# A four-layer graph network on one core: gated sums of two destination tiles in one addition, and staging drained as high parts, counts, low parts

## What is computed

```python
h = relu(layernorm(x))
g = sigmoid(h @ W_gate + b_gate)                    # one gate for a node
x = x + segment_sum(edge_weight * (g * (h @ W))[dst], src)     # layer 0, the weighted one
x = x + segment_sum(h[src], dst) @ W1.T + b1                   # layer 1, h of the new x
x = x + concat(h, segment_sum(message(h[src], h[dst]), dst)) @ W_upd + b_upd   # layer 2
x = x + relu(batchnorm(D_inv * A @ (B_inv * A.T @ (h @ W3)) + b3))             # layer 3
```

## Time and profile before

| what | value |
|---|---|
| time, median of 3 runs | 2575.72 us (2571.42 to 2576.82) |
| the profiled execution: its own time | 2590.25 us |
| the profiled execution: span from the first to the last instruction | 2588.4 us |
| the build, as a stretch of the span | 131.8 to 1327 us |
| mean granted TensorE clock | 0.958 of full speed |
| bytes moved by DMA | 589.27 MB, mean 228 GB/s |

### The profile page before, as it was taken

One profiled execution on the slowest core, in us unless ns is written; L12 is line 12 of the kernel. 1 busy time (PEld: TensorE's weight loads), 2 busy tenths in 40 slices (PEclk: granted clock), 3 DMA queues, 4 the chain that ended last, 5 costly groups with the idle time before them and its releaser, 6 DMA issues. The chain is left out here.

```text
span 2588.4 us, 71075 instructions
## 1 busy us (share of the span) xinstructions
PE 2311.7 (89%) x27901; PEld 1993.6 (77%) x27901; DVE 1599.1 (62%) x3654; ACT 1218.6 (47%) x2644; POOL 45.6 (2%) x51
## 2 busy tenths in 40 slices
PE   2489899999989998999938999899998999999997
PEld 2368788878778887887837888788887888887786
DVE  6689999999999998999962333234433222122223
ACT  2478787877778886887732222222232000011112
POOL 3300000000000000000000000000000000000000
PEclk9589999999999999999979999999999999999998
DMA  6579999999999999999999999899997999999997
GB/s 190 110 152 204 208 208 207 215 217 210 201 193 216 213 213 201 196 215 209 207 229 232 283 284 281 227 260 259 260 258 203 290 288 290 274 246 245 256 267 186
DMA packets 1608975, 589.27 MB, mean 228 GB/s; under 512 B 964422, under 2 KB 1605450, under 8 KB 1608567
## 3 DMA queue, kind: packets, MB, share of 16 engines
q1 hardware_dynamic: 1604869, 579.88, 100.7%
q0 software_dynamic: 1600, 4.92, 0.7%
q10 hardware_dynamic: 2226, 0.62, 0.2%
HBM read 255.26 MB, written 89.20 MB: 133 GB/s over the span
## 5 line engine op out<-in xcount | busy, mean ns | idle before, releaser
L1182 ACT CAST stage<-ps 128x784 f16<-128x784 f32 x784 | 656.5, 837 | 108.5 <-DMA counts_by_source<-stage 69.5
L655 PE MATMUL ps<-Ha,a_tiles 128*128 128x258 f16 x4802 | 548.2, 274 | 46.4 <-ACT Ha L1229 38.9
L655 PEld LDWEIGHTS ps<-Ha,a_tiles 128*128 128x128 f16 x4802 | 469.9, 98 | 116.5 <-ACT Ha L1229 39.1
L608 PE MATMUL ps<-hot_c,hot_r 128*128 128x98 f16 x3136 | 509.8, 212 | 13.6 <-DVE hot_c L890 7.3
L609 PE MATMUL ps<-hot_c,hot_r 128*128 128x98 f16 x3136 | 504.1, 211 | 0.0
L610 PE MATMUL ps<-hot_c,hot_r 128*128 128x98 f16 x3136 | 502.3, 210 | 0.0
L1167 ACT CAST stage<-ps 128x392 f16<-128x392 f32 x784 | 398.8, 509 | 141.5 <-PE ps L591 141.5
L583 PE MATMUL ps<-g_in,wt 128*128 128x128 f16 x2401 | 431.4, 222 | 34.7 <-DVE X L902 18.2
L584 PE MATMUL ps<-g_in,wt 128*128 128x128 f16 x2401 | 429.4, 222 | 0.0
L585 PE MATMUL ps<-g_in,wt 128*128 128x128 f16 x2401 | 429.2, 222 | 0.0
L902 DVE SCALAR_TENSOR_TENSOR X<-ps,X 128x512 f32<-128x512 f32 (+1 forms) x637 | 391.6, 649 | 52.1 <-PE ps L585 51.9
(11 more groups left out here) (195 smaller groups left out, 2039.8 us busy)
## 6 DMA issues: line engine op xcount, KB each, us to landing
a_tiles<-counts_by_source SPq DMA_DIRECT2D x147, 1600.0 KB, 8.8
counts_by_source<-stage SPq DMA_DIRECT2D x49, 1600.0 KB, 8.0
gated_parts<-G SPq DMA_DIRECT2D x7, 448.0 KB, 3.6
g_in<-gated_parts SPq DMA_DIRECT2D x98, 32.0 KB, 3.1
out_x<-X SPq DMA_DIRECT2D x12, 256.0 KB
edge_table<-tab SPq DMA_DIRECT2D x1, 2448.0 KB, 10.5
wt<-stage SPq DMA_TRANSPOSE x98, 10.9
dst_run<-in_dst SPq DMA_DIRECT2D x1, 612.4 KB
```

Source lines behind the costliest of these rows:

```text
L608: mm(into(0), rows_, codes(0), start=v == 0, stop=True, skip_group_check=True)
L655: last = mm(ps[:, c % 2, 0:PARTS], a_slot(ph, c, i), moving[:, i], start=i == 0, stop=i == TILES - 1)
L1182: a.copy(stage[:, b, 0:2, 0:TILES, u * SET_COLS:(u + 1) * SET_COLS], of).then_inc(s("hi_done"), 1)
```

## The change

1. **Two destination tiles in one addition.** `sum_four(n, cp, g)` now works on a pair of tiles (2n and 2n + 1): each of the 4 source tiles gets 6 products in one accumulation, and DVE adds the bank once. Fours 0 to 5 of a pair run in the odd tile 2n + 3 (steps 1 to 6), fours 6 to 12 in the even tile 2n + 4 (steps 0 to 6): one four in a step, not two. Products and bytes stay; additions fall from 637 to 325. The last pair is tile 48 alone.
2. **Buffers.** `wt` becomes 6 half-tile homes (table HOMES), `g_in` 4 slots. To make room, keys and weights no longer stay in SBUF: setup stores them to DRAM (`edge_groups`), and SP loads one group of 128 KB for each pair of tiles into one of two slots (`meta`).
3. **Order and waits of the drain.** `hand_on` now issues: high parts (`g_in`, then transposes of 24 and 25 blocks), the store of the counts, low parts (the same). ACT waits before its first high copy for the store and the high transposes, and for the low transposes only before its first low copy into that half (u = 2).
4. Setup: the waits of DVE for all keys and weights go; it waits for one group when it reaches it.

The core of the diff:

```diff
+FIRST = 6
+HALF_TILES = (range(0, 4 * FIRST), range(4 * FIRST, TILES))
+HOMES = (((0, 1), (2, 3)), ((4, 5), (0, 2)), ((1, 3), (4, 0)), ((5, 2), (1, 4)), ((3, 0), (5, 1)), ((2, 4), (3, 5)))
+def fours_at(c, h):
+    if c % 2:
+        return range(h - 1, h) if 1 <= h <= FIRST else range(0)
+    return range(FIRST + h, FIRST + h + 1) if FIRST + h < FOURS else range(0)
...
+            def store_groups(m):
+                lot = batch(m)
+                sp.wait_ge(s("meta_w"), m + 1)
+                sp.wait_ge(s("keys_in"), 16 * (m + 1))
+                to = groups[lot.start:lot.stop].rearrange("n e x -> e n x")
+                sp.dma_start(to[:, :, 0:KEYS], keys_b[:, m % 2]).then_inc(s("meta_stored"), 16)
+                sp.dma_start(to[:, :, KEYS:], weights_b[:, m % 2]).then_inc(s("meta_stored"), 16)
...
                 def hand_on(j, k, c):
-                    b = c % 2
-                    if later(j, 2):
-                        sp.wait_ge(s("four_done"), (j - 1) * FOURS)
-                    for a, done in enumerate(("hi_done", "lo_done")):
...
-                        sp.dma_start_transpose(wt[:, b, a], stage[:, b, 1 + a, 0:TILES].rearrange("p i d -> p (i d)")).then_inc(s(f"wt_in{b}"), 16)
-                    sp.dma_start(two_tiles(j), stage[:, b, 0].rearrange("p (i a) d -> p i (a d)", a=2)).then_inc(s(f"stored{b}"), 16)
+                    b, pair = c % 2, pair_of(k, c)
+                    if b:
+                        sp.wait_ge(s("hot_ready"), j * TILE_HOTS + TILE_HOTS)
...
+                        sp.dma_start(meta[:, to], of).then_inc(s(f"meta_in{to}"), 16)
+                    if b and later(j, 2):
+                        sp.wait_ge(s("four_done"), (pair - 1) * FOURS + FIRST)
+                    elif later(j, 4):
+                        sp.wait_ge(s("four_done"), (pair - 1) * FOURS)
+                    def turn(a, done, turned):
+                        part = slice(a * P, (a + 1) * P)
+                        sp.wait_ge(s(done), (j + 1) * HALVES)
+                        sp.dma_start(g_in[:, c % 4, part], slab(g_dram, j)[:, part]).then_inc(s(f"g_loaded{b}"), 16)
+                        for half, tiles in enumerate(HALF_TILES):
+                            first = FULL + a * TILES + tiles.start
+                            sp.dma_start_transpose(wt[:, home(c, half), a, 0:len(tiles)],
+                                                   stage[:, b, first:first + len(tiles)].rearrange("p i d -> p (i d)")).then_inc(s(turned), 16)
+                    turn(0, "hi_done", f"hi_turned{b}")
+                    sp.dma_start(two_tiles(j), stage[:, b, 0:FULL].rearrange("p (i a) d -> p i (a d)", a=2)).then_inc(s(f"stored{b}"), 16)
+                    turn(1, "lo_done", f"lo_turned{b}")
...
+                def sum_four(n, cp, g, both=True):
+                    f, e = n * FOURS + g, (cp + g) % 2
+                    if not (isinstance(n, int) and n * FOURS + g < 2):
+                        pe.wait_ge(s("added"), f - 1)
+                    half = int(g >= FIRST)
                     for i in range(4 * g, min(4 * g + 4, TILES)):
                         o = ps[:, 6 + e, (i % 4) * P:(i % 4 + 1) * P]
+                        for b in range(1 + both):
+                            c = 2 * cp + b
+                            at_ = wt[:, home(c, half), :, i - HALF_TILES[half].start]
+                            mm(o, at_[:, 0], g_in[:, c % 4, 0:P], start=i % 4 == 0 and b == 0, stop=False, skip_group_check=True)
+                            mm(o, at_[:, 0], g_in[:, c % 4, P:2 * P], start=False, stop=False, skip_group_check=True)
+                            last = mm(o, at_[:, 1], g_in[:, c % 4, 0:P], start=False, stop=True, skip_group_check=True)
                     last.then_inc(s("four_done"), 1)
```

In the build loop of DVE (first lines) and of ACT (behind the mark):

```diff
-                        t, tb, hh = (j - 2, b, h - 2) if h >= 2 else (j - 3, 1 - b, h + TILE_HOTS - 2)
-                        if not isinstance(t, int) or t >= 0:
-                            for g in summed_at(hh):
-                                add_four(t, tb, g)
+                        back = 1 + (c % 2 == 0 or h < 2)
+                        n, cp = pair_of(k, c) - back, c // 2 - back
+                        for g in fours_at(c if h >= 2 else c - 1, (h - 2) % TILE_HOTS):
+                            if not isinstance(n, int) or n >= 0:
+                                add_four(n, cp, g)
...
                             act.wait_ge(s("low_left"), j * HALVES + (u - 1))
+                            if u == 2 and later(j, 2):
+                                act.wait_ge(s(f"lo_turned{b}"), n * 32)
                             low_parts(*before_at(b, c, u))
                         if u == 0 and later(j, 2):
                             act.wait_ge(s(f"stored{b}"), n * 16)
-                            act.wait_ge(s(f"wt_in{b}"), n * 32)
+                            act.wait_ge(s(f"hi_turned{b}"), n * 32)
```

More of the change, by code:

```diff
@@ L213, in gnn_kernel @@
         base0 = place[0]
[L216 to L217 removed]
+        meta, o = at("meta", [P, 2, GROUP_WORDS], F16, base0)
         iota_r, o = at("iota_r", [P, P, 2], F16, o)
@@ L382, in _ @@
                 turn_keys(m)
+            sp.wait_ge(s("meta_stored"), 32)
+            for n in range(2):
+                sp.dma_start(meta[:, n], groups[n]).then_inc(s(f"meta_in{n}"), 16)
             store_gated(0)
@@ L486, in interleave @@
                 pool.wait_ge(s("weights_turned"), 16 * (m + 1))
-                lot = batch(m)
-                pairs = meta_w[:, lot.start * P // 2:lot.stop * P // 2].rearrange("p q a b -> p a q b")
-                g.tensor_copy(pairs, turned_w[:].rearrange("p a (q b) -> p a q b", b=2)).then_inc(s("meta_w"), 1)
+                if m >= 2:
+                    pool.wait_ge(s("meta_stored"), 32 * (m - 1))
+                to = weights_b[:, m % 2].rearrange("p n (q a b) -> p a n q b", q=P // 2, b=2)
+                for a in range(WEIGHTS):
+                    last = g.tensor_copy(to[:, a], turned_w[:, a].rearrange("p (n q b) -> p n q b", n=BATCH, b=2))
+                last.then_inc(s("meta_w"), 1)
             def high_parts(c):
@@ L625, in build @@
                         half_windows(j, c % 2, c, 2 * h + 1)
-                        if later(j, 2):
-                            sums(j - 2, c % 2, k * (SLOTS // 2) + c // 2, h)
+                        for g in fours_at(c, h):
+                            if not isinstance(n, int) or n >= 0:
+                                if g == 0:
+                                    loaded(n, 0)
+                                    loaded(n, 1)
+                                sum_four(n, cp, g)
                 if general:
@@ L635, in layers @@
                         take_high(0, TILES - 1, u)
-                    for t in (TILES - 2, TILES - 1):
-                        for h in range(TILE_HOTS):
-                            sums(t, t % 2, t // 2 + 1, h)
+                    for n in (GROUPS - 2, GROUPS - 1):
+                        for b in range(1 + (n < GROUPS - 1)):
+                            loaded(n, b)
+                        for g in range(FOURS):
+                            sum_four(n, n, g, n < GROUPS - 1)
                 for ph in (1, 2, 3, 4):
```

109 lines of the change are left out of this document (60 added, 49 removed).

## The result

The changed kernel takes **2585.09 us** (median of 10 runs, 2576.84 to 2588.78), the one before in the same session 2575.91 (median of 10, one of which, at 4598.36 us, stands outside the state of the others and is left out of the ratio). The ratio is 1.0039, with a 95% interval of 1.0028 to 1.0051 (the two medians alone give 1.0036): slower by 0.4%, where 2523 us, 52.5 us less, was forecast. The profiled execution is the fastest of the ten (2576.84 us, span 2575.0, clock 0.954), so it stands 8 us under the median; the one of before stood 14 us above its own.

What follows compares the result with a forecast made beforehand. DVE bounds the build at 23.1 us a tile, then SP at 22.4: 154.0 + 1075.2 + 10 + 36 gives 1275 instead of 1327.5, 52.5 us less than 2575.72, so 2523 us; range 2474 to 2572.

Steps and rivals of the forecast that it cites:

- What bounds the kernel now: Build: DVE bounds at 23.1 us a tile, PE and ACT need 21.2; ACT's 69.5 us of store waits are stalls.
- Additions: DVE in the build: 637 additions become 325, 3.7 us less a tile, at most 2.7 us of it usable.
- The drain on SP: SP's issues per tile: a load held 4.83 us behind the store, splits free, making SP's period 22.4 us.
- Bytes: DMA engines in the build: three 1,600 KB transfers a tile take 16.6 us at 290 GB/s, under either period.
- Waits of ACT: ACT in the build: the 69.5 us store wait goes; low parts land at 24.8 us, wanted at 24.6, just fitting.
- The stalls stay: Rival, build: low parts land slightly late and PE pauses each tile; period 23.1, 20 us less, 2555 us; chance 0.17.
- Setup: Before the build: stores ahead of the weights' transpose delay DVE's first one-hot by 2 us, bounds 0 and 5.
- End: After the last hand-over: remaining fours put the next layer's loads 36 us later, where it was 30.4.
- The 10 us of pauses: Build, where the loop jumps back: of 16 us of PE pauses, 10 remain in the sum.
- each transfer has a fixed part: Rival, drain: two added seams a tile at 1.3 us each; period 25.0, 69.5 us more, 2645 us; chance 0.12.
- PE's floor: Rival, build: SP is not held and PE bounds; period 21.4, 97 us less, 2479 us; chance 0.25.
- signs of being wrong: Build: load behind the store issued in 0.4 us, 24 blocks much over 3.9 us, or PE's clock under 0.97.

Runs made afterwards that it cites:

- e7: Kernel before, with only 1 of 25 parts of the counts stored during the build, full stores behind it; period 23.21 us, 2805.31 us in all (single run).
- e2: Changed kernel, with only 1 of 25 parts of the counts stored during the build, full stores behind it; period 21.60 us, 2728.78 us in all (single run).
- e9: Kernel before, with only each 49-block transpose split into 24 and 25 blocks; 2601.53 us, ratio 1.0086 to the kernel before.
- e4: Kernel before, with only the new drain order and separate waits, transposes whole and old additions; 2576.45 us, ratio 1.0004 to the kernel before.
- e1: Changed kernel, with the store of the counts moved behind both pairs of transposes; 2613.51 us, ratio 1.0158 to the kernel before.
- e11: Changed kernel, with the counts stored twice, the second time to an array of their own; period 29.06 us, 2845.32 us in all (single run).
- e6: Changed kernel, with one load of `g_in` ahead of the high pair, so low transposes stand directly behind the store; 2586.46 us, ratio 1.0038 to the kernel before.
- e3: Changed kernel, with the store of the counts issued on ACT's queue; 2622.11 us, ratio 1.0183 to the kernel before.
- e8: Changed kernel, with the store of the counts issued on GpSimd's queue; period 25.88 us, 2683.57 us in all (single run).
- e10: Changed kernel, with 19 of 25 parts of the store in the build, full stores behind it; period 22.60 us, 2780.91 us in all (single run).

## Why the prediction was wrong

*What bounds the kernel now.* DVE's 23.1 us a tile, PE's and ACT's 21.2 and the list of issues were read rightly; e7 and e2 give 23.2 and 21.6. What was not read is a **second limit at nearly the same height**. The prediction put the 69.5 us of the earlier trace rows down as stalls. They were the sign that the drain already filled the period: its issues end 16.9 us after the hand-over (median) and the store lands 8.0 us after its own, about 25 in all against DVE's 23.1, so that the lone wait was the drain's limit touching DVE's.

*Additions.* 325 of them, DVE idle for 9.2 of 49 us (4.5 us a tile; 3 were forecast): right. They are worth 1.6 us a tile, and only without the store.

*The drain on SP: the step that failed.* The prediction's period of 22.4 us is the term that was too small: SP's first issues are 23.77 us apart (143.42 to 1284.45). From tile 0 to tile 48 that makes 1141 us where 1085 were forecast (48 x 22.4 and 10 of pauses), 56 of the 62 us between 2523 and 2585. That SP would be held behind the store, and that its chain would be the new bound, was right. The terms of the chain against the measured means: high transposes 7.88 with their load, measured 8.12 and 0.4 for the load; hold 4.83, measured 4.53; low transposes 7.86, measured **9.10**. By these differences 22.4 becomes 22.4 + 0.6 - 0.3 + 1.2 = 23.9, near the 23.77. The low pair holds most of the miss, and its two parts can be seen one at a time:

| low pair, us | whole (49 blocks) | split (24 + 25) |
|---|---|---|
| store behind it | 7.84 (before) | 8.39 (e9) |
| store ahead of it | 8.47 (e4) | 9.10 (changed) |

The split adds 0.6, the store ahead of the pair adds 0.6 to 0.7, and both add up. That the second part is the tail of the store is argued from the first of the two low transposes, which has all of it: 4.88 us in the mean for 24 blocks, where e1 with nothing ahead has 4.03. The prediction priced the split at nothing, by the 10-block transposes, and gave the low transposes the median of all, 7.86, with no share for the store ahead of them. The only transpose that it could see behind a held load, at 174.52 in the earlier trace rows, took 7.43 (its other row, 7.41, has no store ahead of it). The first tiles are not the mean of 49: e4, whose transposes are whole, gives 8.47.

*Bytes.* "DMA engines are cover, if a thin one", 16.6 us at 290 GB/s, was the same error. The rate of 290 belongs to a backlog; transposes fed by SP, with the store between them, need 8.1 + 5.4 + 9.1 with issues between, and the DMA share was 1.09 in both kernels. The row of 218 GB/s was at hand and was not put into the sum: 4.8 MB at 218 are 22.0 us, above the floor. That is an upper estimate, since the store itself moves faster (25 parts in 5.35 us by e11, about 300 GB/s).

*Waits of ACT.* The wait for the store went, as forecast. The fit of the low parts, 24.8 to 24.6, was short by 0.2 even in the prediction's own numbers, and it did not hold: the issue alone ends 25.1 us after the hand-over at the median (21.8 was forecast), and the landing comes behind it. That gives the new wait of 79.9 us. "The stalls stay" named this wait, but with DVE's 23.1 as the period and not the drain's.

*Setup.* In the four profiles with the old setup the hand-over of tile 0 ends at 151.9 (the one shown), 137.9 (e4), 140.8 (e7) and 139.3 (e9), so that 11 to 14 us of the profile of before were its own. In the nine with the new setup it ends at 143.3 to 145.6. The new setup costs about 5 us; 2 were forecast, with bounds of 0 and 5.

*End.* From SP's last hand-over to the loads of layer 1 36.2 us, forecast 36, and 30.4 before: right. The 10 us of pauses were right as well, as far as the floor shows them: where the loop jumps back the hand-overs of e2 are 27.2 and 26.1 us apart and not 21.5, 10.3 us in sum.

*Rivals.* The one that came true in sign is "each transfer has a fixed part". Its deciding point, a period of 23.5 or 0.55 us a seam, was well placed: e9 measured 0.6 a split, and the period passed 23.5. Its price of 1.3 was too high, and it had a chance of 0.12; the other half of the miss, the slower transposes behind the store, is in none of the rivals. The fixed 2.0 us in a DMA that the Trainium skill gives ("DMA: Bandwidth & Descriptors", section "Anatomy of one DMA", a fit for DMAs that GpSimd issues) is not seen in SP's time in a split here either: 0.6. "PE's floor" is excluded by the hold, which is there in every tile (3.57 to 5.57 us). Of the prediction's own signs of being wrong, the load was held, but the 24 low blocks took 4.88 us, much over 3.9 (the high ones 3.92), and the clock of the build fell to 0.96, under 0.97.

*The account.* Against before with 14 us of unusual setup taken off (2574.4, the setup of e4), the profiled execution of after (span 2575.0) has 5 us more up to the hand-over of tile 0, 7 less from there to that of tile 48, 9 more to the loads of layer 1 (SP begins the last tile 3 us late, and the end proper is 6 longer), and 6 less in layers 1 to 3: in sum 1. The profile of e6, which lies at its median as that of the changed kernel does not, has +7, 0, +8 and -4, in sum about +10, where the medians give +9. So the changed kernel's usual period is likely that of e6, 23.85. This is an inference, since one execution of each was profiled. The 4 to 6 us in the later layers lie in the last pass, where PE's waits for the transposed loads are smaller (17.3 + 14.1 us before, 10.7 + 8.0 after); e4 (16.8 + 13.4) and e9 do not have it, and e6 has half of it (14.4 + 11.5). Why is open. Not tried: the new additions with unsplit transposes, since four whole-tile homes for `wt` need 25 KB of a partition more than the six half homes, and I saw no room for it. By e4's chain of 22.1 us in place of 23.0 that kernel would have a period of about 22.9, an estimate that no run confirms. Of the kernels that were run, none beats the one before.

## What to carry to other kernels

When the engine that is 100% busy is only a little above a wait for a DMA in the same loop, there are two limits, and relief for one is worth at most the distance to the other. Here DVE's 23.2 was taken away, and the drain, which the change itself made longer by its splits, stood at 23.7. A run with the suspected transfer shrunk to nothing, in both kernels, shows in two profiles what the change is worth and what takes it back. Work out a drain from rates seen while it is fed in that very pattern, not from a backlog's, and count every transfer that is made in two where there was one.

## What the runs showed of the hardware

- The hold behind a store of 1,600 KB does not go away as long as a load or a transpose follows it at once or runs beside it. It appears as a held load (4.53 us), as a longer transpose behind the store (13.91 against 9.10, e6) or as a longer one beside it from another queue (13.01 and 14.04 against 8.12, e3 and e8).
- A low transpose behind the store takes longer even after the held load: 8.47 against 7.84 us whole (e4), 9.10 against 8.39 split (changed, e9).
- Each part of 64 KB in the store adds 0.19 to 0.21 us to the period above the floor (e10, changed, e11).
- Two transposes in place of one cost 0.6 us (e9; 0.3 in the high pair of the changed kernel), though a transpose of 10 blocks takes no more per block than one of 49.
- The granted clock was lower in stretches in which PE did fewer products: 1.00 from 473 with 757, 820 and 757 (before, e2, e7), 0.95 with 733 and 0.90 with 627 in the changed kernel. It is not the number alone: before it was 0.96 with 656.
